# Two gated 3x3 convolutions: a flat padded layout for the moving operand, and blocks of nine row pairs for the second convolution

## What is computed

```python
def qconv_cg(x, w, theta):
    yp = conv(x[:, :16], w[:, :16])
    yr = conv(x[:, 16:], w[:, 16:])
    return yp + sigmoid(2.0 * (yp - theta)) * yr
h   = relu(bn(qconv_cg(x, w_a, theta_a)))
out = relu(x + bn(qconv_cg(h, w_b, theta_b)))
```

## Time and profile before

| | us |
|---|---|
| median of 3 runs | 467.6 (467.1 to 467.66) |
| the profiled execution | 467.52 |
| its span, first to last instruction | 465.7 |
| busy: PE matmul / PE weight load | 452.9 / 444.1 |
| busy: DVE / ACT | 256.0 / 222.1 |

### The profile page before, as it was taken

The page is one execution under the profiler, slowest core; times in us unless marked ns, Lnnn a source line. Parts: engine busy times, 40 slices in busy tenths (PEclk is TensorE's granted clock), DMA queues, the critical chain, the costliest instruction groups (busy, mean ns, idle before and its releaser), DMA issues.

```text
span 465.7 us, 17751 instructions
## 1 busy us (share of the span) xinstructions
PE 452.9 (97%) x8233; PEld 444.1 (95%) x8233; DVE 256.0 (55%) x423; ACT 222.1 (48%) x348; POOL 6.9 (1%) x20
## 2 busy tenths in 40 slices
PE   4999999999999999999999999999999999999994
PEld 4899999999999999999999999999999999999993
DVE  6316655565655565555656565555555565555553
ACT  5226645454544545454544444454545454434332
POOL 5000000000000000000000000000000000000000
PEclk9999999999999999999999999999999999999997
DMA  9930000801526051080605342080333003012315
GB/s 166 219 57 1 4 4 1 140 3 30 114 43 100 4 121 21 4 141 6 136 3 99 45 98 45 3 140 3 67 76 65 9 3 72 1 23 51 72 37 104
DMA packets 116394, 27.13 MB, mean 58 GB/s; under 512 B 116192, under 2 KB 116192, under 8 KB 116320
## 3 DMA queue, kind: packets, MB, share of 16 engines
q1 hardware_dynamic: 115408, 25.86, 30.1%
q10 hardware_dynamic: 592, 0.13, 0.1%
q0 software_dynamic: 320, 0.00, 0.0%
HBM read 13.14 MB, written 12.85 MB: 56 GB/s over the span
## 4 chain that ended last, share of the span: by engine, by line
PE 95%; DMA 2%; ACT 1%; DVE 1%; issue 0%; ACTq 0%
PE acc L323 94%; DMA out_dram<-rows_out 1%; PE acc L287 1%; DMA w_nat<-in_L_conv_w_a_dram 1%; DVE rows_out L545 0%; ACT rows_out L441 0%; ACT L422 0%; ACT mix L422 0%; DVE w_pad L460 0%; ACT w_hi L380 0%; DVE mix L524 0%; ACT x_hi L395 0%; DVE w_pad L458 0%; ACTq L414 0%
## 5 line engine op out<-in xcount | busy, mean ns | idle before, releaser
L323 PE MATMUL acc<-h_hi,w_hi 32*128 32x448 f32 x1392 | 226.7, 367 | 0.0
L323 PE MATMUL acc<-h_lo,w_hi 32*128 32x448 f32 x1392 | 226.6, 367 | 0.0
L323 PE MATMUL acc<-h_hi,w_lo 32*128 32x448 f32 x1392 | 226.5, 367 | 0.0
L323 PE MATMUL acc<-x_hi,w_hi 32*128 32x448 f32 x1344 | 224.4, 374 | 0.8 <-ACT w_hi L380 0.8
L323 PE MATMUL acc<-x_lo,w_hi 32*128 32x448 f32 x1344 | 224.0, 373 | 0.0
L323 PE MATMUL acc<-x_hi,w_lo 32*128 32x448 f32 x1344 | 223.9, 373 | 0.0
L323 PEld LDWEIGHTS acc<-h_hi,w_hi 32*128 32x128 f32 x1392 | 188.3, 184 | 1.2
L323 PEld LDWEIGHTS acc<-h_hi,w_lo 32*128 32x128 f32 x1392 | 188.2, 183 | 1.2
L323 PEld LDWEIGHTS acc<-h_lo,w_hi 32*128 32x128 f32 x1392 | 188.2, 183 | 1.0
L323 PEld LDWEIGHTS acc<-x_hi,w_hi 32*128 32x128 f32 x1344 | 185.5, 188 | 2.7 <-ACT x_hi L395 1.4
L323 PEld LDWEIGHTS acc<-x_hi,w_lo 32*128 32x128 f32 x1344 | 185.8, 188 | 1.3
(11 more groups left out here) (48 smaller groups left out, 30.3 us busy)
## 6 DMA issues: line engine op xcount, KB each, us to landing
x<-in_x_dram SPq DMA_DIRECT2D x30, 392.0 KB, 5.6
out_dram<-rows_out SPq DMA_DIRECT2D x30, 392.0 KB, 6.8
out_dram<-rows_out SPq DMA_DIRECT2D x5, 112.0 KB, 2.5
x<-in_x_dram SPq DMA_DIRECT2D x1, 280.0 KB, 4.8
x<-in_x_dram SPq DMA_DIRECT2D x1, 266.0 KB, 5.5
w_nat<-in_L_conv_w_a_dram SPq DMA_DIRECT2D x1, 144.0 KB, 3.0
w_nat<-in_L_conv_w_b_dram SPq DMA_DIRECT2D x1, 144.0 KB, 4.5
x<-in_x_dram ACTq DMA_DIRECT2D x1, 126.0 KB, 3.1
```

The source lines that it names most:

```text
L323: return pe.matmul(psum[:, bank, 0:N], w[g * ROWS:(g + 1) * ROWS, tap], moving(blk, part, c, dx, g), start=(u == 0 and g in (0, 1)), stop= ...
```

## The change

A slot of the padded tiles becomes 57 elements wide: the zero column at a slot's end is also the one at the next slot's start. A matmul then reads one unbroken run over all slots of its block, the column between them included, whose sums land in PSUM and are skipped when read. An a block stays 8 slots and becomes 456 columns (the seventh of two images is two runs of 228). A b block becomes 9 slots, 9 x 57 - 1 = 512 columns; the ring of 116 slots is 12 such blocks and one of 8 (456 columns). So there are 52 b blocks, 48 of them with 512 columns, where there were 58 with 448. ACT and DVE read PSUM in runs of 56 with steps of 57. The order of blocks is now found by a rule: a b block follows an a block as soon as the last a block that it needs stands 6 places back (`MARGIN`); when the a blocks are used up, only b blocks follow. There are 56 + 52 = 108 blocks and 18 x 108 + 42 = 1986 steps.

```diff
@@ -20,10 +20,11 @@
 
 GR = 16
 ROWS = 2 * GR
-BLK = 8
+BLK, BLK_B = 8, 9
 YR_BANKS, YP_BANKS = 5, 3
 LAG = (42, 0, 21, 42)
 XH_IMGS, X_IMGS, H_IMGS, OUT_IMGS, MIX = 4, 6, 4, 2, 4
+MARGIN = 6
 AHEAD = 4
 
 
@@ -33,25 +34,19 @@
     assert C == GROUPS * GR and GROUPS * ROWS == P and B % 2 == 0
     SLOTS = H // 2
     XS = SLOTS + 1
-    PADW = W + 2
-    N = BLK * W
+    PITCH = W + 1
     HALF = BLK // 2
-    assert N <= BANK and SLOTS == 3 * BLK + HALF and (B * XS) % BLK == 0
     HRING = H_IMGS * XS
-    assert HRING % BLK == HALF
+    assert BLK_B * PITCH - 1 <= BANK and SLOTS == 3 * BLK + HALF and B % H_IMGS == 0
 
 
     A_PAIR = 7
-    NA, NB = B // 2 * A_PAIR, B * XS // BLK
-    LEAD = A_PAIR
-    order = [("a", n) for n in range(LEAD)]
-    for n in range(max(NA - LEAD, NB)):
-        if n < NB:
-            order.append(("b", n))
-        if n + LEAD < NA:
-            order.append(("a", n + LEAD))
-    place = {blk: n for n, blk in enumerate(order)}
-    TOTAL = len(order)
+    NA = B // 2 * A_PAIR
+
+    b_blocks = [(ring * HRING + t, min(BLK_B, HRING - t))
+                for ring in range(B // H_IMGS) for t in range(0, HRING, BLK_B)]
+    NB = len(b_blocks)
+    assert all(k >= BLK for t, k in b_blocks)
 
     def a_slots(n):
 
@@ -66,27 +61,43 @@
 
     def a_needed(m):
 
-        places = [divmod(t, XS) for t in range(BLK * m, BLK * m + BLK + 1)]
+        t, k = b_blocks[m]
+        places = [divmod(t, XS) for t in range(t, t + k + 1) if t < B * XS]
         return max(a_of(img, s - 1) for img, s in places if s) + 1
 
     def b_pieces(m):
 
-        t0 = BLK * m
-        if t0 % HRING == HRING - HALF:
-            runs = [(0, t0 + HALF, HALF), (HALF * W, t0, HALF)]
-        else:
-            runs = [(0, t0, BLK)]
-        cut = []
-        for col, t, n in runs:
-            while n:
-                k = min(n, X_IMGS * XS - t % (X_IMGS * XS), OUT_IMGS * XS - t % (OUT_IMGS * XS))
-                cut.append((col, t, k))
-                col, t, n = col + k * W, t + k, n - k
+        t, n = b_blocks[m]
+        col, cut = 0, []
+        while n:
+            k = min(n, X_IMGS * XS - t % (X_IMGS * XS), OUT_IMGS * XS - t % (OUT_IMGS * XS))
+            cut.append((col, t, k))
+            col, t, n = col + k * W, t + k, n - k
         return cut
 
-    def b_done(img):
-
-        return -(-XS * (img + 1) // BLK)
+    def b_done(img, slot=XS):
+
+        return sum(t < XS * img + slot for t, k in b_blocks)
+
+
+    order, place = [], {}
+    for n in range(NA + NB):
+        na = sum(kind == "a" for kind, m in order)
+        nb = len(order) - na
+        ready = nb < NB and na >= a_needed(nb) and place["a", a_needed(nb) - 1] + MARGIN <= n
+        blk = ("b", nb) if na == NA or ready and order[-1][0] == "a" else ("a", na)
+        place[blk] = n
+        order.append(blk)
+    TOTAL = len(order)
+
+    def slots_of(blk):
+
+        kind, n = blk
+        return b_blocks[n][1] if kind == "b" else BLK
+
+    def leading(blk):
+
+        return 0 if slots_of(blk) == BLK_B else 1
 
 
     CHUNKS = ((0, BLK + 1), (BLK + 1, 2 * BLK + 1), (2 * BLK + 1, XS))
@@ -109,11 +120,13 @@
             return ctx.enter_context(nc.semaphore(name))
 
         x32 = sb("x32", [P, X_IMGS * XS, W])
-        x_hi = sb("x_hi", [P, XH_IMGS, XS, PADW], F32R)
-        x_lo = sb("x_lo", [P, XH_IMGS, XS, PADW], F32R)
-        h_hi = sb("h_hi", [P, HRING + 1, PADW], F32R)
-        h_lo = sb("h_lo", [P, HRING + 1, PADW], F32R)
-        mix = sb("mix", [P, MIX, N])
+
+
+        x_hi = sb("x_hi", [P, XH_IMGS, 1 + XS * PITCH + 1], F32R)
+        x_lo = sb("x_lo", [P, XH_IMGS, 1 + XS * PITCH + 1], F32R)
+        h_hi = sb("h_hi", [P, 1 + (HRING + 1) * PITCH + 1], F32R)
+        h_lo = sb("h_lo", [P, 1 + (HRING + 1) * PITCH + 1], F32R)
+        mix = sb("mix", [P, MIX, BLK_B * W])
         rows_out = sb("rows_out", [P, OUT_IMGS * XS, W])
 
         w_nat = [sb(f"w_nat{k}", [C, C, TAPS, TAPS]) for k in range(2)]
...
@@ -137,7 +150,8 @@
         shift = sb("shift", [P, 2])
         gate_bias = sb("gate_bias", [P, 2])
 
-        psum = ctx.enter_context(nc.psum_tensor("acc", [P, 8, BANK], F32))
+        psum_flat = ctx.enter_context(nc.psum_tensor("acc", [P, 8 * BANK], F32))
+        psum = psum_flat[:].rearrange("p (b n) -> p b n", n=BANK)
 
         w_landed = [sem(f"w_landed{c}") for c in "ab"]
         prm_landed = sem("prm_landed")
@@ -173,11 +187,32 @@
         out_ready = sem("out_ready")
         out_stored = [sem(f"out_stored{n}") for n in range(OUT_IMGS)]
 
-        def yr_bank(b):
-            return psum[:, b % YR_BANKS, 0:N]
-
-        def yp_bank(b):
-            return psum[:, YR_BANKS + b % YP_BANKS, 0:N]
+        def slots(tile, t, k):
+
+            return tile[:, 1 + t * PITCH:1 + (t + k) * PITCH].rearrange("p (s w) -> p s w", w=PITCH)
+
+        def rows_of(bank, blk):
+
+            first, k = bank * BANK, slots_of(blk)
+            if leading(blk):
+                at = psum_flat[:, first:first + k * PITCH]
+            elif bank:
+                at = psum_flat[:, first - 1:first - 1 + k * PITCH]
+            else:
+                return psum_flat[:, 0:k * PITCH].rearrange("p (s w) -> p s w", w=PITCH)[:, :, :W]
+            return at.rearrange("p (s w) -> p s w", w=PITCH)[:, :, 1:]
+
+        def yr_rows(b):
+            return rows_of(b % YR_BANKS, order[b])
+
+        def yp_rows(b):
+            return rows_of(YR_BANKS + b % YP_BANKS, order[b])
+
+        def mixed(b):
+            return mix[:, b % MIX, 0:slots_of(order[b]) * W]
+
+        def mix_rows(b):
+            return mixed(b).rearrange("p (s w) -> p s w", w=W)
 
         def in_middle(tile, n):
 
...
@@ -249,7 +284,7 @@
                 if img < B - 1:
                     store(img)
 
-            ends = [n * BLK - XS * (B - 1) for n in range(NB - 3, NB + 1)]
+            ends = [t + k - XS * (B - 1) for t, k in b_blocks[-4:]]
             for s0, s1 in zip([0] + ends, ends):
                 store(B - 1, s0, s1)
             sp.wait_ge(out_stored[0], 32 * (B // OUT_IMGS))
@@ -267,10 +302,12 @@
                 pool.dma_start(prm_rows[n:n + 1, :], v.rearrange("(a c) -> a c", a=1)
                                ).then_inc(prm_landed, 16)
             for n, t in enumerate((h_hi, h_lo)):
-                nc.gpsimd.memset(t[:, :, 0:PADW:PADW - 1].bitcast(F32), 0.0).then_inc(hpads_zero, 1)
+                nc.gpsimd.memset(t[:, 0:1].bitcast(F32), 0.0)
+                nc.gpsimd.memset(t[:, 1::PITCH].bitcast(F32), 0.0).then_inc(hpads_zero, 1)
 
                 pool.wait_ge(hpads_zero, 2 * n + 1)
-                nc.gpsimd.memset(t[:, 0:HRING + 1:XS, :].bitcast(F32), 0.0).then_inc(hpads_zero, 1)
+                nc.gpsimd.memset(slots(t, 0, HRING + 1)[:, 0:HRING + 1:XS, :].bitcast(F32), 0.0
+                                 ).then_inc(hpads_zero, 1)
 
         @block.tensor
         def _(pe):
@@ -293,22 +330,29 @@
             weights(0, 6)
 
             def moving(blk, part, c, dx, g):
+
                 kind, n = blk
                 rows = slice(g * ROWS, (g + 1) * ROWS)
+                back = 1 - leading(blk)
                 if kind == "a":
                     tile = (x_hi, x_lo)[part]
                     parts = a_slots(n)
                     img, s, k = parts[0]
-                    at = img % XH_IMGS
+                    at = back + (s + c) * PITCH + dx
                     if len(parts) == 1:
-                        return tile[rows, at, s + c:s + c + k, dx:dx + W]
-                    return tile[rows, at:at + 2, s + c:s + c + k, dx:dx + W]
-                tile = (h_hi, h_lo)[part]
-                t = BLK * n % HRING
-                if t == HRING - HALF:
-                    halves = tile[rows, c:c + HRING].rearrange("p (a b) w -> p a b w", b=HALF)
-                    return halves[:, 0::HRING // HALF - 1, :, dx:dx + W]
-                return tile[rows, t + c:t + c + BLK, dx:dx + W]
+                        return tile[rows, img % XH_IMGS, at:at + k * PITCH]
+                    return tile[rows, img % XH_IMGS:img % XH_IMGS + 2, at:at + k * PITCH]
+                t, k = b_blocks[n]
+                at = back + (t % HRING + c) * PITCH + dx
+                return (h_hi, h_lo)[part][rows, at:at + k * PITCH - back]
+
+            def sums(bank, blk):
+
+                kind, n = blk
+                to = psum[:, bank, 0:slots_of(blk) * PITCH - 1 + leading(blk)]
+                if kind == "a" and len(a_slots(n)) == 2:
+                    return to.rearrange("p (i w) -> p i w", i=2)
+                return to
 
             UNITS = 2 * TAPS * 3
 
...
@@ -419,18 +463,18 @@
                         act.wait_ge(hlo_ready, m + 1)
                     else:
                         act.wait_ge(resid_ready, m + 1)
-                nc.scalar.activation(mix[:, b % MIX], yp_bank(b), ACT.Sigmoid, scale=ALPHA,
+                nc.scalar.activation(mix_rows(b), yp_rows(b), ACT.Sigmoid, scale=ALPHA,
```

(23 more changed lines are left out.)

## The result

463.36 us (462.99 to 464.1, 4 runs) against 467.35 us (466.98 to 467.66) before: a ratio of 0.9917, interval 0.9900 to 0.9934, so 4.0 us faster. Forecast were 454 us, 13.6 us faster. The direction was right; the gain is less than a third of the forecast.

What follows compares the result with a forecast made beforehand. PE's matmul steps bound the kernel, with 23.3 ns a step blamed on broken operand runs. Terms -14.7 (steps), +0.3 (low clock) and +0.8 (wait) sum to -13.6 us on 467.5: 454 us forecast, range 430 to 478.

Steps and rivals of the forecast that it cites:

- the 23.3 ns: Part of each 210 ns PE step beyond 186.7 ns for 448 columns, put down to reading the moving operand in runs.
- A step's length: PE step: before 186.7 + 8 x 2.9 = 210 ns; after, one run's cost left, 216.2 ns (512 columns) and 192.9 (456).
- the extra stays: Rival, chance 0.20: 23.3 ns per matmul or a fixed rate per column remains, breaks cost nothing; 493.3 or 499.4 us.
- Its sentence on runs at even starts: In that rival: runs of 56 floats on even starts always hit each 16-byte line twice, so breaks cost nothing.
- Lockstep: PE's four row groups step together, each step lasting as long as its longest matmul; rival without lockstep, chance 0.07, 432.8 us.
- the smaller terms: Additions to PE's sum: +0.3 us for wider columns at the low clock and +0.8 us waiting for h near the end.
- The sum for PE: Steps past the first 55: before 2039 x 0.210 = 428.2 us, after 1761 x 0.2162 + 170 x 0.1929 = 413.5, so -14.7 us.
- +0.3 us: At the start, 55 low-clock steps with 8 more columns each: +0.4 us at most, put at +0.3 us.
- The new order's wait: Near the end, a b block four places behind the last a block makes PE wait for h rows: +0.8 us.
- ACT and DVE: An a and a b block take ACT 6.99 us against 7.8 us on PE, so hidden with 0.8 us to spare.

Runs made afterwards that it cites:

- at 60: Kernel before with slots of 60 elements in place of 58, still 8 runs of 56: 469.38 us, ratio 1.0054, 211.5 ns a step.

## Why the prediction was wrong

**What bounds the kernel: right.** PE's steps set the end before and after, and the 23.3 ns beside the array's time were rightly put into the supply of the moving operand of one row group: it is not the loads (loads of half the columns change nothing), nor what groups share (the last block with two groups has the same 208 ns), and with two-byte elements all but 3 ns of it is gone.

**A step's length: the step that failed first.** I took the 23.3 ns for 8 runs at 2.9 ns and left one. No row had an unbroken read at the high clock, and I chose "the only thing in the operand's read that comes eight times". Breaks cost nothing. The cost goes by 16-byte pieces, and four float32r columns need one piece whether the run is broken or not; 1.75 ns is just over the 1.67 that four columns are at 2.4 GHz. Unbroken steps were to be 192.9 and 216.2 ns, with 2.9 left of the 23.3; they are 208 and 232 to 233 ns, with 18 to 19 left. What the layout can save is the pieces at gaps: 116.25 against 114.5 of them, measured 2.3 ns of 210. In the changed kernel the padding column that is now read takes back hardly any of that (it lies in a piece that is touched anyway; 208.0 against 207.7 ns) but costs time at the low clock, where columns count: (20.80 - 18.52) / 6 = 0.380 us a step, 0.373 before.

```profile
18.52 2.65 PE L367 MATMUL acc<-x_hi,w_lo 32*128 32x456 f32 x12
20.80 1.72 PE L367 MATMUL acc<-x_lo,w_hi 32*128 32x456 f32 x7
```

The rival "the extra stays" (0.20) had it right that breaks cost nothing, and its steps were nearer than the forecast's: 213.3 and 236.6, or 213.8 and 240.0, against 208 and 233. Its sentence on runs at even starts left out that a third of the taps start at odd ones.

**Lockstep: the step that failed second.** I read the fixed order of starts as a bond. With equal blocks it would look so in any case, so the row could not tell; the start at 15.88 us could, and I made no use of it. With unequal blocks the groups drift within the three steps that `LAG` leaves, and the mean of 208 and 233 counts. The two errors had opposite signs, and that the direction came out right is luck: the gain comes from the distance of 57, to which the forecast gave no price, and the real steps in lockstep would have made 486 us (1761 x 0.233 + 170 x 0.208 = 445.7 us for PE, 17.5 more than 428.2, and 1.1 for the smaller terms, on 467.5). The run with one step of slack, 481 us, comes near that.

**The sum for PE** is 1931 x 0.2201 = 425.0 us, the wait near the end included, against 428.2 before: -3.2 us, forecast -14.7. The last matmuls end at 453.13 + 1.40 = 454.5 us, before at 457.40 + 1.43 = 458.8, so 4.3 us apart, as the spans are (461.4 and 465.7). Some 0.4 us of what the sum lacks lies at the start: the step length shows the clock up at 28.00 us in place of 29.48, about six steps fewer at the low clock, where +0.3 us was forecast. Counted start by start, step 54 comes at 29.0 us in place of 29.5. Why the clock came up earlier is not shown. The rest lies in steps outside the window. The new order's wait was forecast at +0.8 us and costs 1.1. ACT and DVE stayed hidden, as worked out.

**Nines.** Six blocks fewer save 6 x 18 times the 6 to 10 ns beside the pieces, 0.6 to 1.1 us, and the order that comes with them cost 1.1 us until `MARGIN` was raised. Both versions with the least time, 461.84 us (ratio 0.9894) and 461.73 us (0.9890), are 1.1 and 1.3 us ahead of the changed kernel, at the edge of what the intervals tell apart: the changed kernel with `MARGIN` 9, and the kernel before with slots 57 apart and nothing else. The two can't be told from each other.

**Open.** Why at 60 the tap at shift 2 takes 0.22 us and that at shift 1 0.21 us, though both touch 120 pieces; why a contiguous run of 448 takes 207 ns and 112 aligned runs of four 203, with 112 pieces each; why the price of a piece comes out at 1.3 ns between 57 and 59; whether the rest of 5 to 10 ns is one thing. The two-image blocks, two runs of 228, were not measured apart. How far the groups might drift without the waits was not tried.

## What to carry to other kernels

When TensorE reads float32r, count the 16-byte pieces that a matmul's moving operand touches: at 2.4 GHz they, more than the columns, set the pace here, and a layout that packs rows closer or aligns short runs gains while the number of runs hardly matters. When a trace has only one kind of item, an order that is always the same says nothing on whether it is enforced; ask what unequal items would do, and measure it by taking the slack away. And try the smallest part of a change by itself: here one number, 58 to 57, gave all of the gain.

## What the runs showed of the hardware

At 2.4 GHz a float32r moving operand costs about 1.75 ns per 16-byte piece touched (1.73 to 1.77 over wide differences, 1.3 between slots 57 and 59 apart) and 5 to 10 ns a matmul: a 32-row matmul of 448 contiguous columns takes 207 ns and one of 456 columns 208, against 193 for 456 columns of bfloat16. Moving runs of four by eight bytes took the same matmul from 203 to 397 ns. Row groups on one array run at different paces at the same time (0.21 and 0.232 us a step), and matmuls of two groups start out of program order (15.88 us in the kernel before). At the low clock of 1.2 GHz a step is the columns alone, 0.373 us for 448 and 0.380 for 456.
